# Scan stage of a two-layer graph kernel: row chunks of 512, pair sums by transfers, small steps at other places

## What is computed

```
h = relu(layernorm(x))
x = x + relu(normalised_adj(adj) @ h @ W.T + b)            # layer 0
h = relu(layernorm(x))
x = x + mamba(layernorm(relu(adj @ h @ gcn_w + gcn_b)))    # layer 1

# mamba, over the L = 8192 rows in order:
xc, z = h @ w_in                     # 256 columns each
u  = silu(causal_conv4(xc) + conv_b)
dt, B, C = split(u @ w_xp);  dt = softplus(dt @ w_dt + b_dt)
hst = exp(dt * A) * hst + dt * B * u # 256 x 16 states, a recurrence over rows
y  = (sum over the 16 states of hst * C + u * D) * silu(z)
out = y @ w_out
```

## Time and profile before

| | us |
|---|---|
| median of 3 runs | 2611.35 (2610.81 to 2611.61) |
| the profiled execution, whole | 2612.32 |
| its span, first to last instruction | 2610.5 |
| stage C, ahead of the first slot (1384.8 to 1464.4) | 79.6 |
| chunks 0 to 12 (1464.4 to 2392.3) | 927.9 |
| chunks 13 to 15 (2392.3 to 2594.2) | 201.9 |
| behind the last scan | 16.3 |

### The profile page before, as it was taken

One profiled execution on the slowest core, in us unless ns is written; L12 is line 12 of the kernel. 1 busy time (PEld: TensorE's weight loads), 2 busy tenths in 40 slices (PEclk: granted clock), 3 DMA queues, 4 the chain that ended last, 5 costly groups with the idle time before them and its releaser, 6 DMA issues.

```text
span 2610.5 us, 21684 instructions
## 1 busy us (share of the span) xinstructions
PE 2222.9 (85%) x6736; PEld 1251.9 (48%) x6736; DVE 2085.1 (80%) x2087; ACT 978.6 (37%) x1696; POOL 1067.6 (41%) x461
## 2 busy tenths in 40 slices
PE   0436889999999999999999988889988988886776
PEld 0212334444457888888885434444444443443333
DVE  7899998888527656656652599999999999999997
ACT  0100000000015555555551455555555555555552
POOL 0000000000000000000000499999999999998554
PEclk9968899999999999999999989999999999997898
DMA  9999999989756556555556656665656565562221
GB/s 393 417 421 422 421 418 387 391 360 381 276 214 237 207 201 225 189 215 201 198 181 243 240 202 220 207 215 214 214 204 227 206 223 194 215 210 69 69 73 53
DMA packets 108322, 642.99 MB, mean 246 GB/s; under 512 B 14224, under 2 KB 15024, under 8 KB 42672
## 3 DMA queue, kind: packets, MB, share of 16 engines
q1 hardware_dynamic: 92160, 604.02, 61.4%
q10 hardware_dynamic: 16048, 37.57, 4.0%
HBM read 625.28 MB, written 16.25 MB: 246 GB/s over the span
## 4 chain that ended last, share of the span: by engine, by line
PE 55%; DVE 24%; DMA 8%; issue 8%; ACT 4%; DVEq 0%; ACTq 0%; SPq 0%
PE ps L848 21%; PE ps L767 14%; PE ps L888 10%; DVE ps L685 6%; DVE arena L590 6%; DMA ring<-adj 5%; DVE arena L700 5%; PE ps L966 4%; DVE ring L700 3%; DMA arena<-adj 2%; PE ps L917 2%; PE ps L909 1%; PE ps L970 1%; DVE parts L726 1%; PE ps L928 1%
## 5 line engine op out<-in xcount | busy, mean ns | idle before, releaser
L458 POOL TENSOR_TENSOR rstd<-base,minus_half 128x8 f32<-128x8 f32 (+1 forms) x40 | 84.7, 2118 | 1406.4 <-DVE base L510 811.7
L848 PE MATMUL ps<-adj_parts,h_parts 128*128 128x512 f32 x2592 | 593.6, 390 | 2.6 <-ACT adj_parts L1062 2.2
L888 PE MATMUL ps<-ring,diag_h 128*128 128x512 f32 x1152 | 566.2, 627 | 0.9 <-DVE arena L672 0.9
L848 PEld LDWEIGHTS ps<-adj_parts,h_parts 128*128 128x128 f32 x2592 | 484.7, 188 | 109.0 <-ACT adj_parts L1062 4.7
L590 DVE TENSOR_TENSOR arena<-arena,ring 128x2048 f32<-128x2048 f32 x180 | 412.6, 2292 | 57.9 <-DMA ring<-adj 47.2
L767 PE MATMUL ps<-ring,arena 128*128 128x512 f32 x824 | 381.9, 622 | 53.1 <-DMA ring<-adj 53.0
L474 POOL TENSOR_TENSOR arena<-arena 128x1024 f32<-128x1024 f32 x156 | 377.6, 2431 | 67.7 <-ACT state L1129 67.6
L700 DVE TENSOR_TENSOR_SCAN arena<-arena,state,ps 128x512 f32<-128x512 f32 x312 | 382.4, 1267 | 28.6 <-ACT arena L1137 8.7
L888 PEld LDWEIGHTS ps<-ring,diag_h 128*128 128x128 f32 x1152 | 229.5, 201 | 254.1 <-issue 248.9
L609 DVE TENSOR_TENSOR adj_parts<-ring,adj_parts 128x1024 fp32r<-128x1024 f32 x216 | 264.0, 1225 | 94.5 <-ACT adj_parts L1062 83.7
L1137 ACT ACTIVATE arena<-arena,a_sb 128x512 f32<-128x512 f32 x512 | 338.4, 708 | 0.4
(11 more groups left out here) (97 smaller groups left out, 2095.5 us busy)
## 6 DMA issues: line engine op xcount, KB each, us to landing
ring<-adj SPq DMA_DIRECT2D x452, 1024.0 KB, 6.6
arena<-c_scratch SPq DMA_DIRECT2D x128, 512.0 KB, 4.2
diag_h<-adj SPq DMA_DIRECT2D x32, 1024.0 KB, 12.6
arena<-adj SPq DMA_DIRECT2D x28, 1024.0 KB, 16.1
arena<-x ACTq DMA_DIRECT2D x16, 512.0 KB, 6.0
x_scratch<-arena ACTq DMA_DIRECT2D x8, 512.0 KB, 3.0
arena<-x_scratch ACTq DMA_DIRECT2D x16, 256.0 KB, 5.4
out<-arena ACTq DMA_DIRECT2D x16, 256.0 KB, 3.7
```

The costliest lines, as they stand in the source:

```text
L848: last = nc.tensor.matmul(acc[:, c, :], h_parts[:, blk % 2, layer, h_part, a * F:(a + 1) * F], adj_parts[:, buf, adj_part, c * MM:(c + 1) ...
L888: last = nc.tensor.matmul((acc_c if i else y_ps)[:, c, :], tile_of(h1, JT * s + a), blk[:, a * STRIP + c * MM:a * STRIP + (c + 1) * MM], s ...
```

## The change

All of it but the layout of the blocks and a few steps of the layernorms lies in stage C.

1. **Products by chunk.** `adj` blocks are laid out in halves of 512 rows; a load of stage C is two such halves (1 MB, 4 KB pieces). The unit is (chunk, pair of blocks, j), with an accumulator bank per chunk, `s1` of 512 columns in three buffers, and a rule that deals the products: 24 stand ahead of the slots (was 32), 8 in the first slots, none until slot -6, then evenly to slot 214 (was 204). The first two chunks take layer 1's upper sum straight from `l1_stage`.
2. **POOL.** In the 13 chunks with quads, the second pair of a quad is added to the first by an accumulating transfer of 128x2048 from SBUF to SBUF, issued by POOL (three a chunk; POOL waits for it three slots later, then does one add). The last quad of a chunk is added as before. POOL also takes w and the gate from DVE, and for each layernorm the scale and nmr (four small instructions in the place of one).
3. **DVE.** The small steps stand between the product and the scans of their slot. The statistics are spread over four slots. The split reads PSUM instead of the copy `bcv`. L510, L514, w and the gate are gone from DVE.
4. **ACT and SP.** `da` has three buffers and is made two slots ahead; `csb` has three and is loaded two slots earlier. New stage offsets, among them GCN -24 (was -19) and OUT 30 (was 25).

```diff
-GCN, BIAS, STATS, POWER, NORMALISE = -19, -19, -17, -17, -15
-TRANSPOSE, XZ, SILU, DBC, SPLIT = -13, -12, -7, -6, -5
-DT, SOFTPLUS, WEIGHTED_U = -4, -3, -1
-QSUM, NSUM = 7, 6
-LOAD_X1, SKIP, GATE, OUT, RESIDUAL = 12, 20, 21, 25, 25
+GCN, BIAS, STATS, AGGREGATE, NORMALISE = -24, -23, -22, -18, -17
+TRANSPOSE, XZ, SILU, DBC, SPLIT = -13, -12, -8, -7, -6
+DT, SOFTPLUS, WEIGHTED_U = -5, -4, -3
+QSUM, NSUM = (9, 9, 9, 7), 6
+LOAD_X1, SKIP, GATE, OUT, RESIDUAL, STORE = 22, 20, 21, 30, 31, 32
...
+    units = {k: [(k, p, j) for p in pairs_of[k] for j in range(PJ)] for k in range(NCH)}
+    ahead = BPS // 2 * PJ
+    products[FIRST_SLOT - 1] = units[2][:ahead] + units[3][:ahead] + units[0]
+    rest = units[1] + units[2][ahead:] + units[3][ahead:] + [unit for k in range(4, NCH) for unit in units[k]]
...
+    for g in range(FIRST_SLOT, end):
+        due += (len(rest) - n - due) / (end - g) if g > DBC else n < len(units[1])
+        while due >= 1 - 1e-6 and n < len(rest):
...
-        da = [work2(HALVES, T) for _ in range(2)]
+        da = [work2(HALVES, T) for _ in range(3)]
...
-        csb = [work2(2, T) for _ in range(2)]
+        csb = [work2(2, T) for _ in range(CSB)]
...
+            def norm_scale(m, cols):
...
+                nc.gpsimd.tensor_scalar(nmr[:, 0:cols], mv[:, 0:cols, 0], -1.0, None, ALU.mult)
+                nc.gpsimd.tensor_scalar(base[:, 0:cols], mv[:, 0:cols, 1], LN_EPS, None, ALU.add)\
+                    .then_inc(pool_step, 1)
+                pool.wait_ge(pool_step, next(pool_steps))
+                nc.gpsimd.tensor_tensor(rstd[:, 0:cols], base[:, 0:cols], minus_half[:, 0:cols], ALU.pow)\
+                    .then_inc(pow_done, 1)
+                pool.wait_ge(pow_done, m + 1)
+                nc.gpsimd.tensor_tensor(nmr[:, 0:cols], nmr[:, 0:cols], rstd[:, 0:cols], ALU.mult)\
+                    .then_inc(norm_ready, 1)
...
+                    nc.gpsimd.tensor_tensor(w[k % 2], dt[k % 2], u[k % 2], ALU.mult).then_inc(w_ready, 1)
...
+                    nc.gpsimd.tensor_tensor(yg, yg, sz[k % 2], ALU.mult).then_inc(yg_ready, 1)
...
+                    k, n = divmod(g, DS)
+                    if k < QUAD_CHUNKS and n % 4 == 2 and n >= 6:
+                        q = g // 4 - 1
+                        pool.wait_ge(quad_in, 16 * (q - k + 1))
+                        first, second = (hs[(4 * q + j) % HSB] for j in range(2))
+                        nc.gpsimd.tensor_tensor(first, first, second, ALU.add).then_inc(quad_done, 1)
+                    if k < QUAD_CHUNKS and n % 4 == 3 and n < DS - 4:
+
+                        pool.wait_ge(mult_done, g + 1)
+                        pool.dma_start(hs_pairs[(g // 2 - 1) % (HSB // 2)], hs_pairs[g // 2 % (HSB // 2)],
+                                       accum_op=ALU.add).then_inc(quad_in, 16)
+                    if k < QUAD_CHUNKS and n % 2 and n >= DS - 4:
...
+                k = chunk_at(g, SPLIT)
+                if k is not None:
+
+                    dve.wait_ge(bc_high, k + 1)
+                    low = parts[k % 2][LOW:KD, :]
+                    nc.vector.tensor_tensor(low, misc_of("dbc", k)[LOW:KD, :], low.bitcast(F32), ALU.subtract)\
+                        .then_inc(misc_free, 1)
```

368 lines of the change are left out of this document (198 added, 170 removed).

## The result

The changed kernel takes 2567.41 us (median of four executions, 2558.74 to 2570.38), the kernel before 2611.44 beside it. The ratio is 0.9824, 95% interval 0.9809 to 0.9839: faster by 44 us (1.8%), where 99 were forecast. The times lie inside the range, but the mechanism that was to give them does not hold in full. The executions of the changed kernel differ by 12 us from one another, those of before by 0.8.

A forecast was written before the change was run, and what follows sets the result against it. DVE led stage C before, POOL was to set the pace after: 2612.3 - 19.8 (preparation) - 14.7 (last chunks) + 1.1 + 13 (66.3 - 71.4) = 2512.6, 2512 us on the median's scale; 8 in 10: 2470 to 2590.

The forecast's parts named there:

- DVE's own work: Chunks 0 to 12: DVE falls from 71.4 to 62.6 us a chunk through moved steps, the split, placing and fewer waits.
- The issue of a transfer: POOL, chunks 0 to 12: 1.2 us for each of three issues, +3.6 a chunk (1.0 to 7.1).
- Rival (b): POOL's small costs at their upper bounds (issues 2.36 each, layernorm step +1.9): 71.7 us a chunk, 2582 us; chance 0.18.
- Rival (c): Adding transfer outlasts POOL's three slots; gain gone at 12.8 us a transfer, 2737 us at 16; chance 0.10.
- cost at nothing: Stages A and B: block layout and a few tiny layernorm steps have slack, costed at nothing, bounded by some us each way.
- c = 66.3: Mean time of a chunk in chunks 0 to 12, set by POOL: 63.8 us plus 2.5 of waits for transfers; was 71.4.
- The term of the transfers: POOL's waits for transfers in chunks 0 to 12: 2.5 us a chunk at 9.5 us a transfer (0 to 9.6).
- the forecast's own rule: A transfer must land within POOL's work of three slots: 9.4 us for a chunk's first, 7.1 second, about 11.7 third.
- DVE with PE at 64.2: Chunks 0 to 12: DVE's 62.6 us plus 1.6 of new waits in PE's heavy slots (0 to 4) a chunk.
- No cover to spare: PE's slot 3 waits for POOL's last quad (slot 15), about 11 us late, so POOL's extra time shows.
- rival (a): Transfer hidden, landing within 7.1 us, issue under 1 us: DVE with PE bounds at 64.2, 2485 us; chance 0.26.
- the last three chunks: Chunks 13 to 15: DVE counts, as POOL is busy only 122.4 of 201.9 us; -14.7 us (-9 to -18).

The follow-up runs named there:

- e4: Changed kernel with the 39 adding transfers undone, POOL adding every pair and quad itself: 2623.25 us, ratio 1.0039 to the kernel before.
- e1: Changed kernel with the layernorm steps of stages A and B as before (POOL only the power, DVE base and nmr): 2550.73 us, ratio 0.9762.
- e9: Changed kernel with each adding transfer moving 128 of 2048 elements a row (64 KB), the rest of those sums left out: 2531.6 us.
- e19: Changed kernel with stage C's adj loads cut to 256 KB of each 1 MB, adding transfers whole: 2537.19 us.
- e2: Changed kernel with skip and residual behind the scans again in chunks 13 to 15: 2564.39 us.
- e7: Changed kernel with all of PE's pair sums in the last three chunks one slot earlier (NSUM 5): 2563.59 us.
- e11: Changed kernel with the last pair sum and last adj products of the chunks without quads, and every chunk's output product, one slot earlier: 2569.46 us.
- e17: Changed kernel with stages A and B's layernorm as before, and PE's last pair sum and output product one slot earlier in the last three chunks: 2543.67 us.
- e8: Changed kernel with POOL's four layernorm instructions behind the product and add of their slot, ACT's normalise a slot later: 2575.43 us.
- e10: Changed kernel with the third quad of a chunk added by POOL, leaving two transfers a chunk: 2610.83 us, ratio 0.9987.
- e13: Changed kernel with the skip and the gate one slot later, nothing else: 2587.08 us.
- e14: Changed kernel with the third quad added by POOL, and skip, gate and PE's sum of the fourth quad a slot later: 2597.81 us.
- e3: Changed kernel with w back on DVE, behind the scans of slot 15: 2562.09 us.
- e5: Changed kernel without the 39 adding transfers and their waits, so those sums lack the second pair of three quads a chunk: 2526.45 us.

## Why the prediction fell short

**Right.** The sign, by the transfers: e4 shows that without them nothing is gained. The preparation: 59.1 against 59.8 forecast. DVE's own work: 67.8 less 5.7 of waits is 62.1, forecast 62.6; so gate, w, base, nmr, the split and the placing were sized well in their sum. The 38 us of PE at the second dt product are gone. The stretch behind the last scan: 1.6 for 1.1. The issue of a transfer: 0.90 us, and 0.30 of wait for POOL's own product ahead of each, together the 1.2 forecast (bounds 0.33 and 2.36). Rival (b) has no part in the result, since the small steps are 0.20 to 0.24 us in stage C and pow 1.04. Rival (c) didn't come either: 11 to 12 us is above the 9.5 taken and below the 12.8 from which it decides.

**Wrong, first: stages A and B "cost at nothing".** 15 us, by e1. The step said that the layernorm has slack there; I read no row for it. The chain ran through one more engine for three more instructions, and ACT, which waits for it, feeds PE at 1.00 of its clock with nothing to spare. It was outside the sum and outside the range's reasons. The pow alone took 2.52 us there where it takes 1.75 in the kernel before and in e1; why isn't shown.

**Wrong, second: c = 66.3, measured 67.8.** The term of the transfers was right in size (2.5 us a chunk for the waits; e9 and e19 give 2.4), but by luck, and it was put on the wrong base. By the forecast's own rule (9.4, 7.1 and 11.7 us to hide a transfer in) a landing of 11.8 us, a usual one here, costs POOL 2.4 + 4.7 + 0.1 = 7.2 us a chunk. POOL waited 1.8, nearly all at the second quad, as the rule had it: it was lighter, and it idles 5.2 us a chunk for ACT's state copy where 2.4 were kept, so that a transfer has longer to land. The time that the waits cost came by another way, through DVE's slot n=2 and PE's slow sum. The working took the larger of two engines, DVE with PE at 64.2 and POOL at 63.8 + 2.5. POOL turned out lighter by 2.1 a chunk (59.3 with the issues, forecast 61.4) and yet its wait for a transfer went straight into the time, because DVE is the leader, loses it in slot n=2, and a lost slot isn't caught up. So it is a sum, not a maximum: 65.2 to 65.5 without the waits (forecast 64.2) plus 2.4. The missing 1.0 to 1.3 of the base are PE's picks, 2.2 us a chunk even in e19 and 2.6 in the changed kernel instead of 1.6 for all of PE, and 0.6 at the split, which was sized as if ACT's step ahead of it took nothing. "No cover to spare" in slot 3 was the right warning at the wrong place: the late quad is the third, not the fourth. (A smaller slip: gcn moved five slots earlier, not three; the 38 us went as forecast.)

Of the transfer's time, the trace shows 10.9 to 12.3 us to landing. It takes 22.9% of 881.8 us in 39 transfers, 5.2 us of all 16 DMA engines each, beside q1's 61.3%; with q1 at 34% it lands in 9.3 to 10.4. The Trainium skill, "DMA: Bandwidth & Descriptors", in its section on the anatomy of a DMA from the gpsimd path, gives 2.0 us plus bytes/436e3, an estimate of 4.4 us for a plain copy of 1 MB; by it rival (a), 2484, would have held. No run has an adding transfer of 1 MB near that, with much traffic beside it or with less, so for these the measured time decides.

**Wrong, third: the last three chunks, -14.7 forecast and +3.2 measured.** The step "POOL is busy for 122.4 of 201.9 us, so DVE counts" forgot PE, because it priced the placing of small steps as a gain (0.21 us each) and nothing else. A step between product and scans that needs PE's newest result stops the whole slot; behind the scans it had 2.5 us of cover. e2, e7, e11 and e17 show it: with the sum and the output product one slot earlier, in e17, chunks 14 and 15 take 61.9 and 60.6 us, forecast 62.7 and 60.7. What is left over in e17 is chunk 13 (73 us), with the quads of chunk 12 behind it and a copy that waits for PE's last products in slot n=7.

**What stays open.** No order that I tried in chunks 0 to 12 is shown to be better than the one given: e8, e10, e13 and e14 are slower by 8 to 43 us, e3 is undecided. Why e8 lengthened the landing, and by which step e13's later gate makes slot n=2 longer, isn't settled; in e13 too the transfers land later (10.9 to 13.1 us) and POOL's wait at the second quad grows from 20.9 to 36.3 us. Why the third quad added by POOL costs 3 us a chunk isn't shown either. How PE's granted clock and the late quads depend on each other is read from the rows alone: no run changes the clock by itself.

## What to carry to other kernels

A step moved into a tight place between two others of the leading engine must have its input a full slot earlier; check each for what it waits for, not only for how long it runs. Where the leading engine loses time at a fixed step, the waits of the engines that follow add to its chunk and don't hide under the largest sum. A wait can do its harm far from where it stands: look back from the late step along its engine to the last idle time. Work that is moved to a less busy engine in a stage "with slack" still lengthens the chain through it: look for who waits for the last instruction of that chain before it is costed at nothing.

## What the runs showed of the hardware

An adding transfer of 1 MB from SBUF to SBUF took 5.2 us of the 16 DMA engines, 4.9 a MB, where the loads of q1 took 2.9 a MB (61.3% of 881.8 us for 189 MB); the like of 64 KB landed in 5.6 to 7.0 us, so about half of the landing was there at a sixteenth of the size. Issuing one costs POOL 0.90 us, at 64 KB as at 1 MB. POOL's pow on 8 columns took 2.52 us in stage B of the changed kernel and 1.75 at the same place in e1; on 4 columns, in stage C, it took 1.92 before and 1.04 after. Behind the issue of a chunk's third transfer POOL's w took 2.64 us on the mean, 2.57 with transfers of 64 KB, and 2.35 to 2.36 where that transfer was missing (e5, e10). Four products of PE took 3.78 us at a granted clock of 0.50, after 4.38 us of idle, and 1.98 in another chunk of the same stage. Executions of the changed kernel spread by 12 us where those of before spread by 0.8. The transfers can't be the whole reason: e4, which has none, spreads by 9.1 and e5 by 5.5.
